# Pipeline fill of a fused Perceiver block: value weights ahead of x, low parts on VectorE, scores between query tiles

## What is computed

```python
def xattn(q, k, v):                      # 16 heads of 32; q = layernorm(x), k = v = ctx
    qh, kh, vh = q @ Wq + bq, k @ Wk + bk, v @ Wv + bv
    attn = softmax(einsum('blhe,bshe->bhls', qh, kh) / sqrt(32))
    return einsum('bhls,bshd->blhd', attn, vh) @ Wo + bo

x = x + xattn(layernorm(x), ctx, ctx)
x = x + linear_attention(layernorm(x))   # 16 heads, 128 features each
x = x + moe_ffn(layernorm(x))            # 16 experts, top 8 tokens each per batch, and a shared FFN
```

## Time and profile before

| | us |
|---|---|
| median of 3 runs | 710.9 (710.53 to 712.37) |
| the profiled execution, its own time | 712.38 |
| its span | 710.6 |
| TensorE busy | 671.1 (94%) |
| VectorE busy | 286.3 (40%) |
| ScalarE busy | 240.1 (34%) |
| GpSimd busy | 42.7 (6%) |

### The profile page before, as it was taken

The page is one execution under the profiler, slowest core; times in us unless marked ns, Lnnn a source line. Parts: engine busy times, 40 slices in busy tenths (PEclk is TensorE's granted clock), DMA queues, the critical chain, the costliest instruction groups (busy, mean ns, idle before and its releaser), DMA issues.

```text
span 710.6 us, 10423 instructions
## 1 busy us (share of the span) xinstructions
PE 671.1 (94%) x4272; PEld 428.4 (60%) x4272; DVE 286.3 (40%) x595; ACT 240.1 (34%) x468; POOL 42.7 (6%) x43
## 2 busy tenths in 40 slices
PE   6699999999999999799998889999999999999996
PEld 5477777787877776478976474444444444444532
DVE  4845636445364354775876752111111111111112
ACT  4455536455453443355782122111111111111110
POOL 1800000000000000381000100000000000000000
PEclk9999999999999999999999999999999999999999
DMA  8111010110610000303076803899999999999911
GB/s 312 57 60 60 2 61 6 55 60 1 250 48 2 0 2 2 103 1 130 0 296 281 372 0 119 302 403 377 408 355 404 374 384 369 376 387 378 378 64 61
DMA packets 14348, 129.69 MB, mean 183 GB/s; under 512 B 2720, under 2 KB 2848, under 8 KB 6240
## 3 DMA queue, kind: packets, MB, share of 16 engines
q1 hardware_dynamic: 12384, 127.09, 46.2%
q10 hardware_dynamic: 1920, 1.97, 0.9%
HBM read 126.03 MB, written 1.05 MB: 179 GB/s over the span
## 4 chain that ended last, share of the span: by engine, by line
PE 82%; DVE 10%; ACT 4%; issue 1%; DMA 1%; SPq 1%; ACTq 1%; DVEq 0%
PE ps L959 23%; PE ps L1206 15%; PE ps L1238 8%; PE ps L1213 7%; PE ps L1245 4%; PE ps L1127 4%; PE ps L1032 4%; PE ps L1005 2%; PE ps L1043 2%; PE ps L1227 2%; PE ps L1164 2%; PE ps L1071 2%; PE ps L1176 1%; DVE stats L642 1%; DMA x<-in_x 1%
## 5 line engine op out<-in xcount | busy, mean ns | idle before, releaser
L855 DVE TENSOR_TENSOR hid<-hid,ps 128x256 f32<-128x256 f32 (+1 forms) x32 | 17.6, 553 | 141.6 <-PE ps L1206 91.4
L585 ACT ACTIVATE hid<-ps 128x256 f32<-128x256 f32 (+1 forms) x32 | 15.7, 490 | 141.6 <-PE ps L1213 86.5
L1238 PE MATMUL ps<-w_d,hid_T 128*64 128x512 f32 x256 | 58.4, 598 | 1.4 <-ACT hid_T L600 1.4
L1206 PE MATMUL ps<-w_u,x_slot 128*64 128x512 f32 x256 | 58.4, 598 | 0.0
L1206 PE MATMUL ps<-w_g,x_slot 128*64 128x512 f32 x256 | 57.8, 593 | 0.0
L476 ACT ACTIVATE probs<-ps,neg_max 128x512 f32<-128x512 f32 x64 | 43.5, 687 | 36.3 <-DVE neg_max L723 36.3
L959 PE MATMUL ps<-wv_hi,ctx_hi 128*128 128x512 f32 x128 | 52.3, 408 | 2.9 <-POOL wv_lo L395 2.9
L959 PE MATMUL ps<-wv_lo,ctx_hi 128*128 128x512 f32 x128 | 50.7, 396 | 0.0
L959 PE MATMUL ps<-wv_hi,ctx_lo 128*128 128x512 f32 x128 | 50.5, 395 | 0.0
L702 DVE COPY probs_T<-ps 128x512 f32<-128x512 f32 x32 | 22.1, 692 | 68.7 <-PE ps L1032 68.7
L723 DVE TENSOR_REDUCE neg_max<-ps 128x1 f32<-128x512 f32 x64 | 39.8, 684 | 20.2 <-PE ps L1005 20.2
(11 more groups left out here) (192 smaller groups left out, 1154.3 us busy)
## 6 DMA issues: line engine op xcount, KB each, us to landing
w_u<-in_wu SPq DMA_DIRECT2D x16, 2048.0 KB, 15.9
w_d<-in_wd SPq DMA_DIRECT2D x16, 2048.0 KB, 14.6
w_g<-in_wg SPq DMA_DIRECT2D x16, 2048.0 KB, 10.5
ctx_raw<-in_ctx SPq DMA_DIRECT2D x7, 1024.0 KB, 4.7
w_qkv<-in_wqkv SPq DMA_DIRECT2D x1, 3072.0 KB, 13.6
ws_g<-in_wsg SPq DMA_DIRECT2D x1, 2048.0 KB, 7.7
ws_u<-in_wsu SPq DMA_DIRECT2D x1, 2048.0 KB, 7.7
ws_d<-in_wsd SPq DMA_DIRECT2D x1, 2048.0 KB, 21.1
```

The source lines that it names most:

```text
L1206: ins = pe.matmul(ps[64 * fh:64 * (fh + 1), dst, :], x_slot[:, dt, e, :], weights[e % 2][:, dt, BANK * fh:BANK * (fh + 1)], start=(dt == 0 ...
L1238: ins = pe.matmul(ps[64 * fh:64 * (fh + 1), 6 + n % 2, :], hid_T[:, n % 2, j, 64 * fh:64 * (fh + 1)], w_d[e % 2][:, KT * fh + j, :], start ...
```

## The change

- SP issues wv ahead of x.
- The low parts of wv and wq are computed by VectorE: wv's right after `first_low`, wq's between the layer norm and `xn_low`. GpSimd keeps the bias additions.
- ScalarE: high parts of wv, the first two roots, high parts of wq, all four keys out, the last two roots, three value tiles out, `xn_high`, the last value tile.
- TensorE: V0, V1 and V2 follow the keys, then the transposes, V3, Q0 and Q1, the first half of the scores, Q2 and Q3, the second half of the scores. The queries go to banks 3, 4, 0, 1.
- VectorE: maxima of the first half and two normalisations before Q3 is copied; ScalarE: three exponents before Q2 is copied.
- `xn_lo_cross` and `wq_hi` get space of their own.

```diff
--- before.py
+++ after.py
@@ -85,10 +85,6 @@
 
         k_T = sb(cross, "k_T", [P, KT, S])
         v_s = sb(cross, "v_s", [P, NS, D])
-        first = ExitStack()
-        xn_lo_cross = sb(first, "xn_lo_cross", [P, KT, TOK], F32R)
-        wq_hi = sb(first, "wq_hi", [P, KT, D], F32R)
-        first.close()
         probs = sb(cross, "probs", [P, PAIRS, S])
         first = ExitStack()
         wq_lo = sb(first, "wq_lo", [P, KT, D], F32R)
@@ -102,6 +98,8 @@
         bias_k = sb(cross, "bias_k", [P, KT])
         bias_v = sb(cross, "bias_v", [P, KT])
         bias_q_scaled = sb(cross, "bias_q_scaled", [P, KT])
+        xn_lo_cross = sb(cross, "xn_lo_cross", [P, KT, TOK], F32R)
+        wq_hi = sb(cross, "wq_hi", [P, KT, D], F32R)
         cross.close()
         xn_cross, wk_raw = probs[:, 0:KT], probs[:, KT:2 * KT]
         wq_raw, wv_raw = o_T, v_s
@@ -259,7 +257,7 @@
         SCORE = (5, 6, 7, 2, 5, 6, 7, 3)
         GROUP = PAIRS // 2
         FIRST_K = 4
-        EARLY_V = 2
+        Q_BANK = (3, 4, 0, 1)
 
         LN_BANK, RES_BANK = (2, 4, 0), (0, 4)
         ATT_BANK = (0, 1, 2, 7)
@@ -326,8 +324,8 @@
                 sp.dma_start(ctx_raw[:, dt], ctx_d[0, :, dt]).then_inc(ctx0_in[dt], 16)
             for tile, src in ((bias_k, bk_d), (bias_q, bq_d), (bias_v, bv_d)):
                 sp.dma_start(tile[:], src).then_inc(bias_in, 16)
+            sp.dma_start(wv_raw[:], wv_d).then_inc(wv_in, 16)
             sp.dma_start(x[:], x_d.rearrange("(t p) d -> p t d", p=P)).then_inc(x_in, 16)
-            sp.dma_start(wv_raw[:], wv_d).then_inc(wv_in, 16)
             sp.dma_start(wq_raw[:], wq_d).then_inc(wq_in, 16)
             sp.dma_start(bo_rows[:], bo_d.partition_broadcast(P)).then_inc(rows_in, 16)
             with sp.Fori(1, B) as b:
@@ -390,12 +388,6 @@
                 for t in range(NT):
                     pool.tensor_tensor(x[:, t, :], x[:, t, :], row_bias[:], ALU.add).then_inc(xbias_done, 1)
 
-            for dt in range(KT):
-                pool.wait_ge(w_hi, KT + dt + 1)
-                pool.tensor_tensor(wv_lo[:, dt], wv_raw[:, dt], wv_hi[:, dt].bitcast(F32), ALU.subtract).then_inc(wv_split, 1)
-            for dt in range(KT):
-                pool.wait_ge(w_hi, 2 * KT + dt + 1)
-                pool.tensor_tensor(wq_lo[:, dt], wq_raw[:, dt], wq_hi[:, dt].bitcast(F32), ALU.subtract).then_inc(wq_split, 1)
             pool.wait_ge(rows_in, 16)
             add_row_bias(0, bo_rows)
             pool.wait_ge(xn_done, 2 * NT)
@@ -460,7 +452,7 @@
 
             def q_out(ht):
                 act.wait_ge(q_ps, ht + 1)
-                act.activation(q_T[:, ht, :], bank(2 + ht), ACT.Identity,
+                act.activation(q_T[:, ht, :], bank(Q_BANK[ht]), ACT.Identity,
                                bias=bias_q_scaled[:, ht:ht + 1], scale=HD ** -0.5).then_inc(q_done, 1)
 
             def probs_T_out(b, tiles=range(KT)):
@@ -468,41 +460,43 @@
                     act.wait_ge(pT_ps, b * PAIRS + 2 * ht + 1)
                     act.copy(probs_T[:, ht % 2, 0].rearrange("p s c -> p (s c)"), bank(TRANS[ht % 2][0])).then_inc(pT_done[0], 1)
 
-            def values_and_exponents(b, early=0):
+            def exponent(b, p):
+                act.wait_ge(max_done, b * PAIRS + p + 1)
+                act.activation(probs[:, p, :], bank(SCORE[p]), ACT.Exp, bias=neg_max[:, p:p + 1], scale=1.0,
+                               accum_out=row_sum[:, p:p + 1]).then_inc(exp_done, 1)
+
+            def values_and_exponents(b):
                 for g in range(2):
                     for i in range(GROUP):
-                        p = GROUP * g + i
-                        act.wait_ge(max_done, b * PAIRS + p + 1)
-                        act.activation(probs[:, p, :], bank(SCORE[p]), ACT.Exp, bias=neg_max[:, p:p + 1], scale=1.0,
-                                       accum_out=row_sum[:, p:p + 1]).then_inc(exp_done, 1)
-                        if i >= 2 and 2 * g + i - 2 + early < NS:
-                            v_out(b, 2 * g + i - 2 + early)
+                        exponent(b, GROUP * g + i)
+                        if i >= 2:
+                            v_out(b, 2 * g + i - 2)
 
             first_high()
-            act.wait_ge(bias_in, 48)
-            ln_std(0, (0, 1))
             act.wait_ge(wv_in, 16)
             for dt in range(KT):
                 act.copy(wv_hi[:, dt], wv_raw[:, dt]).then_inc(w_hi, 1)
-            k_out(0, 0, first=True)
-            k_out(0, 1, first=True)
-            ln_std(0, (2, 3))
+            act.wait_ge(bias_in, 48)
+            ln_std(0, (0, 1))
             act.wait_ge(wq_in, 16)
-            act.wait_ge(w_split, KT)
             for dt in range(KT):
                 act.copy(wq_hi[:, dt], wq_raw[:, dt]).then_inc(w_hi, 1)
+            for ht in range(KT):
+                k_out(0, ht, first=True)
+            ln_std(0, (2, 3))
             act.wait_ge(wv_split, KT)
-            v_out(0, 0)
+            for st in range(NS - 1):
+                v_out(0, st)
             xn_high(0)
-            for st in range(1, EARLY_V):
-                v_out(0, st)
-            k_out(0, 2, first=True)
-            k_out(0, 3, first=True)
+            v_out(0, NS - 1)
             ctx_high(1, 1)
             act.wait_ge(bias_scaled, 1)
             q_out(0)
+            for p in range(GROUP - 1):
+                exponent(0, p)
             q_out(2)
-            values_and_exponents(0, EARLY_V)
+            for p in range(GROUP - 1, PAIRS):
+                exponent(0, p)
 
             def step(b, par, more=True):
                 if more:
@@ -693,7 +687,7 @@
 
             def q_out(ht):
                 dve.wait_ge(q_ps, ht + 1)
-                dve.tensor_scalar(q_T[:, ht, :], bank(2 + ht), bias_q[:, ht:ht + 1], HD ** -0.5,
+                dve.tensor_scalar(q_T[:, ht, :], bank(Q_BANK[ht]), bias_q[:, ht:ht + 1], HD ** -0.5,
                                   ALU.add, ALU.mult).then_inc(q_done, 1)
 
             def probs_T_out(b, tiles=range(KT)):
@@ -715,17 +709,23 @@
                 dve.tensor_scalar(probs[:, p, :], probs[:, p, :], row_inv[:, p:p + 1], None,
                                   ALU.mult).then_inc(prob_done, 1)
 
+            def maxima(b, g):
+                dve.wait_ge(score_ps, 2 * b + g + 1)
+                for i in range(GROUP):
+                    p = GROUP * g + i
+                    dve.tensor_reduce(neg_max[:, p:p + 1], bank(SCORE[p]), AX.X, ALU.max,
+                                      negate=True).then_inc(max_done, 1)
+
             def softmax(b):
                 for g in range(2):
-                    dve.wait_ge(score_ps, 2 * b + g + 1)
-                    for i in range(GROUP):
-                        p = GROUP * g + i
-                        dve.tensor_reduce(neg_max[:, p:p + 1], bank(SCORE[p]), AX.X, ALU.max,
-                                          negate=True).then_inc(max_done, 1)
+                    maxima(b, g)
                     for i in range(GROUP):
                         normalise(b, GROUP * g + i)
 
             first_low()
+            for dt in range(KT):
+                dve.wait_ge(w_hi, KT + dt + 1)
+                dve.tensor_tensor(wv_lo[:, dt], wv_raw[:, dt], wv_hi[:, dt].bitcast(F32), ALU.subtract).then_inc(wv_split, 1)
             dve.wait_ge(bias_in, 48)
             dve.tensor_scalar(bias_q_scaled[:], bias_q[:], HD ** -0.5, None, ALU.mult).then_inc(bias_scaled, 1)
             dve.wait_ge(x_in, 16)
@@ -737,11 +737,21 @@
             ln_stats(3)
             ln_rows(0, 2, xn_cross)
             ln_rows(0, 3, xn_cross)
+            for dt in range(KT):
+                dve.wait_ge(w_hi, 2 * KT + dt + 1)
+                dve.tensor_tensor(wq_lo[:, dt], wq_raw[:, dt], wq_hi[:, dt].bitcast(F32), ALU.subtract).then_inc(wq_split, 1)
             xn_low(0, xn_lo_cross)
             ctx_low(1, 1)
             q_out(1)
+            maxima(0, 0)
+            normalise(0, 0)
+            normalise(0, 1)
             q_out(3)
-            softmax(0)
+            normalise(0, 2)
+            normalise(0, 3)
+            maxima(0, 1)
+            for p in range(GROUP, PAIRS):
+                normalise(0, p)
 
             def step(b, par, more=True):
                 if more:
@@ -1006,20 +1016,17 @@
                                         q_T[rows, ht, L * b:L * (b + 1)], k_T[rows, ht, :], start=True, stop=True)
                 ins.then_inc(score_ps, 1)
 
-            def values_and_scores(b, par, first=False):
-
-                early = EARLY_V if first else 0
+            def values_and_scores(b, par):
+
                 for g in range(2):
                     pe.wait_ge(k_done, b * KT + 2 * g + 2)
-                    if g == 0 and first:
-                        pe.wait_ge(q_done, KT)
-                    elif g == 0:
+                    if g == 0:
                         pe.wait_ge(exp_done, b * PAIRS)
                     else:
                         pe.wait_ge(exp_done, b * PAIRS + GROUP - 1)
```

(34 more changed lines are left out.)

## The result

In the first measurement the changed kernel takes 705.83 us (median of 5 runs), the kernel before 712.37 (5 runs): ratio 0.9917, 95% interval 0.9897 to 0.9937. Two later measurements of the same kernel give 0.9907 (0.9889 to 0.9926) and 0.9906 (0.9886 to 0.9927). The profiled executions took 705.49 and 712.38, 6.9 us apart; their spans are 703.7 and 710.6.

The account below looks back on a forecast made before the run. TensorE, carrying 82% of the chain of waits, was taken as the bound. In the fill 10.1 us of holes go and 4.7 come: 5.4 less than the median 710.9 gives 705.5 us, own range 704.6 to 706.5, with rivals 703.3 to 708.3.

Parts of the forecast that it names:

- the rival without a collision: Before the queries: VectorE's wq splits pass GpSimd's additions at no cost, no hole before Q0; gain 7.3 us, 703.6; chance 0.13.
- Steps 1 and 2: Fill: wv lands at 13.9 us, x at 16.3; wv's low parts run 14.6 to 17.1, removing the 3.0 us hole.
- Step 3: Layer norm in the fill: an uncontended tile of rows costs 1.34 us; last rows at 27.3 us, against 31.0 before.
- Step 4: Value matmuls on TensorE: V2 waits for bank 0, freed by ScalarE at 25.5 us, a new hole of 0.6 us.
- Step 5: Before the queries: wq's splits alternate with GpSimd's bias additions, 1.8 us a pair; queries start at 34.8, hole 1.9 us.
- the bound given for no collision: Before the queries, the favourable limit: no hole, with V3 ending at 32.95 us.
- Step 6: Queries and scores: a 1.1 us copy gap before each score half, the second new; batch 1's first keys at 50.5 us.
- The ledger: TensorE's holes before batch 1: 10.1 us go, 4.7 come (0.6, 1.9, 1.1, 1.1), 5.4 us less.
- The slower rival: Clock falls at the hole before Q0 and stays down through 48 query matmuls, costing 9 us: 714.5; chance 0.04.

## Why the prediction was right

**The total** was 705.5 and came at 705.83. That it came so near is luck: the median that it was taken from, 710.9, moved to 712.37 with more runs, 1.5 us up, and the gain was sized about as much too small. Between profiles 5.4 us were forecast and 6.9 measured. By its size alone the gain is nearer to the 7.3 of the rival without a collision; it is the traces that decide against that rival. All but 0.1 of the 1.4 us at K1 come from the hole before V2 (0.6 forecast, none in this profile), the hole before the queries (1.3 for 1.9) and the second gap (1.0 for 1.1).

**Steps 1 and 2** held: wv lands 7.0 us after its issue, ScalarE starts at 13.46 (13.95 forecast), the parts are done at 16.6, the keys' end at 19.57 finds them ready, and the 3.0 us hole is gone. Undoing the issue order alone cost 1.8 to 2.2 us.

**Step 3** held: uncontended rows, 1.29 us a tile where I took 1.34, and with wv's earlier landing they end at 26.5, not 27.3. The reading of *why* this helps was incomplete: I saw late rows as the loss, where the run with V0's copy moved shows rows that end at 29.6 and cost 0.4 us.

**Step 4** named the wait, V2 behind ScalarE's keys and roots, as a hole of 0.6 (0, 0.4 and 0.7 in three profiles). The start of V2 was put at 25.5 and came at 25.04 and 25.22 in the two profiles in which it waited; how much of that is a hole depends on when the keys end. The step missed that the same queue is what makes the move to VectorE pay.

**Step 5**, the collision, was there: splits of 1.78 us in the trace, four in 5.79. The term was mis-sized by the pair, 1.70 in place of 1.8, and by the earlier rows; the queries start at 33.54, not 34.8, a hole of 1.3 (start to start) for 1.9. The run with late additions makes it 0, which was the bound given for no collision.

**Step 6** held to 0.1 us: from the first query matmul to K1 15.6 us against 15.7 forecast, with gaps of 1.1 and 1.0 where 1.1 each were forecast. That the interleaving pays was argued as an exchange of covers only; its own price, 3 us and a fallen clock, came from the run without it.

**The ledger.** 10.1 us of losses before; 1.3, 1.1 and 1.0 after (start to start), so 6.7 by the sum and 6.82 measured. The saving arrived whole. **The slower rival** did not occur: the granted clock is 1.00 in every window from 11.3 to 56, and behind the hole the query matmuls are 0.23 apart. Its price was wrong as well: where a hole of 4.7 us was made at the same place, the clock fell, but it was back after seven matmuls, 1.5 us and not 9.

## What to carry to other kernels

In a pipeline's fill, write the bounding engine's holes down as a ledger from start to start, then follow each hole to the queue that it hangs on: here V2's bank hung on a copy that stood behind roots that wait for statistics. With the low parts on GpSimd, moving that one copy gained 2.2 us at K1, more than the 1.0 to 1.5 of moving the low parts to VectorE. When work goes to another engine, look for what is released by the same event on the engine that it has to take turns with. A gap of one copy's length can be filled with the next batch's first tile, if its own copy is moved forward too.

## What the runs showed of the hardware

VectorE and GpSimd operations with two SBUF inputs each alternated one for one: VectorE splits of 512 went from 0.68 to 1.78 us and GpSimd's additions from 1.25 to 1.7, while VectorE's operations on PSUM ran at their own speed beside GpSimd (four in 2.48). "SBUF — State Buffer" of the Trainium skill, section "SBUF: two separate sides", has the exclusive lock; these runs show that back-to-back streams take turns. Beside GpSimd's splits VectorE's normalisation, with one SBUF tensor in and one out, was stretched as well (1.41 and 1.48 us for 0.55, in the run with V0's copy moved), and so were the two links of the layer norm that take two inputs (1.06 and 1.03 us for 0.22 and 0.16), while the one-input links of the same size stayed at 0.15.

In the runs the clock fell to 1.2 GHz at three holes: of 4.7 us before the queries (granted clock 0.52 from 37 to 39, 0.43 us between the next seven matmuls), of 3.1 us before V2 in the run with wq's low parts on GpSimd (0.57 from 28.54 to 32.10) and of 3.0 us before the second half of the scores (0.50 from 51 to 53). In the kernel before it fell at the hole of 3.2 us before the last transposes. Behind the holes of 2.85 us before V0 in the kernel before, of 2.9 us before V2 with all low parts on GpSimd and of 2.3 us before V2 in the run with x first, the matmuls were 0.23 to 0.24 apart from the second on. Each fall in the runs cost 1.5 us or more beyond the hole itself: 1.5, 1.6, and 2.7 where it took in the scores (0.9) and a tile of keys (1.8).
